# Weights of both layers in one shared pair of buffers, the second layer's prepared in the first layer's last units

## The chip, the cores and the metric

One core of a Trainium2 chip. The metric is the device time of one execution in microseconds, the median of several. Engines: PE (TensorE), DVE (VectorE), ACT (ScalarE), POOL (GpSimd) and SP (SyncE, which here only issues loads and stores).

## What is computed

Two transformer layers on 8 sequences of 256 tokens of 256 numbers, in float32:

```python
xn = _layernorm(x)
x = x + _L0_attn_ref(xn, ...) + _L0_ffn_ref(xn, ...)   # 32 query heads of 8, softmax, memory; 4-bit gated MLP of 2048
xn = _layernorm(x)
x = x + _L1_attn_ref(xn, ...) + _L1_ffn_ref(xn, ...)   # below; ternary gated MLP of 704

# _L1_attn_ref: xc = silu(causal conv of 4 taps over x)
q = _l2n((x @ Wq.T)...); k = _l2n((x @ Wk.T)...); v = _ln((x @ Wv.T)..., vn_g, vn_b)   # 16 heads of 16
i_gate = sigmoid(xc @ ig_w.T + ig_b); gamma = sigmoid(xc @ gamma_w.T + gamma_b)
_, mem = associative_scan(comb, (gamma, i_gate * k * v), axis=1)
o = groupnorm(_ln(mem, mn_g, mn_b) * q) * gn_g + gn_b
return (o * sigmoid(xc @ og_w.T + og_b)) @ Wo.T
# _L1_ffn_ref: quantized = clip(round(w / mean|w|), -1, 1); (sigmoid(x @ q1.T) * (x @ q2.T)) @ q3.T
```

## The kernel before

Float32 products are made of three products of halves: each operand is split into hi (a copy rounded to float32r) and lo (the exact value less hi), and hi*hi, hi*lo and lo*hi are added in PSUM. ACT makes the hi part, DVE or POOL the lo part.

**Layer 0** (`layer0`) runs as one loop over units u = -3 to 67, written out in every engine's queue. Unit u does the attention of head u % 8 of sequence u // 8 (64 in all) and one of 8 chunks of that sequence's MLP, one to three units later (`m = u - LAG`, `down_product(m - BEHIND)`). The weights of the MLP are decoded in the first units into `w_hi` and `w_lo`, [128, 8 pairs, 2, 768]; the last sequence's chunk m = 56 + a is the last reader of pair a. Per unit, PE makes turned scores (`scores_turned`, L832), gate and up (`hidden_product`, L735), scores for the maxima (`scores`, L807), probabilities times V (`weighted`, L847) and down (L874); DVE takes maxima (L595), splits them (`split_max`, L602 and L604), which SP then places by DMA (`place_max`, L251); ACT makes exponentials (L448), hid_hi (L458) and copies (L479); POOL makes hid (L347) and hid_lo (L341). In units 10 to 40 the ternary weights of the second layer are averaged, compared with a threshold and stored as signs (bf16) in `dram["signs"]`. After the last chunk of a sequence DVE adds down to X (step `mlp`, L585) and takes bn_stats (L588).

**Layer 1** (`layer1`) begins, in a block of its own (L985 to L1061), with what it needs once: SP loads the weights of the projections and gates (`l1w`, 1536 KB, L1001), the signs (L1002) and six small tensors (L1010); DVE makes bn_aggr of all 16 tiles, then the centring of the value columns (L1050 to L1056), POOL the reciprocal roots (L1021, L1023), ACT w_hi (L1036) and the ternary weights from the signs (`tern`, L1038) and three small ones (L1040 to L1042), DVE w_lo (L1058) and bias (L1060), POOL scales and wo_lo (L1028 to L1031). The engines meet at the end of each block. Semaphores are primed with 40 (`prime`) so that waits on "zero so far" have positive values.

Then a second block runs five turns, `turns(turn)`, with (late, early, ahead) = (None, 0, 1), (0, 1, 2), (1, 2, 3), (2, 3, None), (3, None, None); the numbers are groups of 512 tokens. I call them turns 0 to 4. In a turn, `ahead` is normalised (DVE, L1434), turned (PE `xn_turn`, L1644), split (ACT `xn_high`, DVE and POOL `xn_low`, L1156) and its convolution begun; `early` gets its projections (PE `query_key`, `value`, L1625; ACT `projected`), norms, gates and up products (`ffn_up`, L1678; ACT sigmoid L1288, DVE `hidden` L1478); `late` gets scan (DVE L1492), memory norm, down products, output norm (`output_normed`), output gate (`gated`, L1145 on POOL for one half and DVE for the other), turn (PE `o_turn`, L1744; ACT o_hi L1348; DVE o_lo L1547), output product (PE `output`, 24 products) and residual (DVE L1553). The queue of each engine is the order of the calls at the end of its `turn`. In PE's: b_turn, ffn_up(0), center_rows, query_key(0), (1), ffn_up(1), query_key(2), value, ... gamma(1), xn_turn(ahead, 0), gate(2), (3), xn_turn(ahead, 1), o_turn, output. On DVE:

```python
if ahead is not None:
    normalise(ahead)
if late is not None:
    output_normed()
if ahead is not None:
    xn_low(dve, ahead, 0)
if late is not None:
    gated(dve, late, 1)
```

## Time and profile before

| | us |
|---|---|
| median of 3 executions | 877.85 (875.49 to 878.04) |
| profiled execution | 876.82 |
| its span, first to last instruction | 874.9 |
| PE busy | 751.2 |
| DVE busy | 649.3 |
| ACT busy | 454.0 |
| POOL busy | 413.9 |
| layer 0, last instruction ends | 606.9 |
| turns begin | 625.5 |
| mean granted clock of TensorE, of full speed | 0.943 |

Times in the rows are microseconds from the first instruction of the profiled execution. A row of the timeline gives start, duration, engine, line, operation, output and inputs with their shapes, the count of merged instructions, and in brackets how long the engine had been idle before it and what released it. PEclk is the granted clock: 1.00 is 2.4 GHz, 0.50 is 1.2 GHz.

### The profile page before, as it was taken

To read this page: it belongs to the slowest core of one execution; us is meant where nothing else is said; L and a number is where in the kernel's file an instruction comes from. 1 tells how busy PE (TensorE), PEld (TensorE's weight loads), DVE (VectorE), ACT (ScalarE), POOL (GpSimd) and SP (SyncE) were. 2 spreads that over 40 slices of the span, in tenths; PEclk is the share of its full clock that TensorE was granted. 3 is DMA by queue.
4 is the path that set the end of the run, shared out by engine and by line. 5 is a ranking of instruction groups with operands and counts; after the bars stand their busy time and mean duration, and the time that the engine had idled before them with its cause. 6 is when DMAs were issued, how large, how long until landed. Compare 5 with 4: busy or idle time off the path is not lost. (4 is left out here: it accounts for less than half of the span.)

```text
span 874.9 us, 15195 instructions
## 1 busy us (share of the span) xinstructions
PE 751.2 (86%) x5602; PEld 648.0 (74%) x5602; DVE 649.3 (74%) x1122; ACT 454.0 (52%) x717; POOL 413.9 (47%) x335
## 2 busy tenths in 40 slices
PE   4268799999999999999999999996267987979773
PEld 3257688888888888888888888885156866858662
DVE  5989877787777677777687686653555898989966
ACT  4346645655756655655655665563554543545411
POOL 1344444254367467576344245334336273762832
PEclk9999999999999999999999999998588897979975
DMA  5011121201001111011000000001200000000000
GB/s 155 24 38 38 37 78 40 57 26 45 19 15 43 32 35 44 21 50 32 3 20 21 2 21 20 3 2 68 91 1 1 1 0 25 1 4 21 0 25 24
DMA packets 21388, 25.88 MB, mean 30 GB/s; under 512 B 4419, under 2 KB 17091, under 8 KB 21061
## 3 DMA queue, kind: packets, MB, share of 16 engines
q1 hardware_dynamic: 21316, 24.93, 9.7%
q8 instruction: 45, 0.74, 0.3%
q14 instruction: 27, 0.21, 0.1%
HBM read 14.83 MB, written 3.28 MB: 21 GB/s over the span
## 5 line engine op out<-in xcount | busy, mean ns | idle before, releaser
L595 DVE TENSOR_REDUCE neg_max<-s_pair 128x4 f32<-128x1024 f32 x127 | 154.9, 1220 | 76.4 <-PE s_pair L807 76.1
L448 ACT ACTIVATE probs<-t_pair 128x1024 f32<-128x1024 f32 x128 | 131.2, 1025 | 139.6 <-PE t_pair L832 139.4
L347 POOL TENSOR_TENSOR hid<-g,hid 128x512 f32<-128x512 f32 x64 | 82.1, 1283 | 179.0 <-DVE g L706 147.5
L341 POOL TENSOR_TENSOR hid_lo<-hid,hid_hi 128x512 fp32r<-128x512 f32 x64 | 85.4, 1335 | 99.0 <-ACT hid_hi L458 98.9
L807 PE MATMUL s_pair<-K,Q 96*128 96x256 f32 x508 | 85.2, 291 | 14.5 <-DVE neg_max L595 9.1
L807 PEld LDWEIGHTS s_pair<-K,Q 96*128 96x128 f32 x508 | 76.0, 195 | 23.1 <-issue 8.5
L832 PE MATMUL t_pair<-Q,K 104*128 104x512 f32 x256 | 85.8, 417 | 0.3 <-DMA Q<-max_parts 0.3
L874 PE MATMUL down<-w_hi,hid_hi 128*128 128x256 f32 x256 | 83.9, 328 | 0.7 <-POOL hid_lo L341 0.7
L874 PE MATMUL down<-w_lo,hid_hi 128*128 128x256 f32 x256 | 72.1, 282 | 0.0
L874 PE MATMUL down<-w_hi,hid_lo 128*128 128x256 f32 x256 | 72.1, 282 | 0.0
L1145 POOL TENSOR_TENSOR rows<-rows,par 128x512 f32<-128x512 f32 x24 | 35.1, 1464 | 75.7 <-DVE rows L1511 54.8
L847 PE MATMUL misc<-probs,V 128*32 128x256 f32 x1024 | 69.1, 388 | 1.5 <-DVE kc L565 1.0
L874 PEld LDWEIGHTS down<-w_hi,hid_hi 128*128 128x128 f32 x256 | 48.2, 188 | 26.4 <-issue 24.3
L735 PE MATMUL gate<-xn_hi,w_hi 128*128 128x256 f32 x256 | 57.0, 304 | 0.0
L698 DVE SCALAR_TENSOR_TENSOR g<-g,gate 128x512 f32<-128x512 f32 x64 | 42.8, 668 | 18.8 <-ACT g L461 18.7
L469 ACT ACTIVATE g<-g 128x512 f32<-128x512 f32 x64 | 40.2, 627 | 29.2 <-DVE g L698 29.2
L735 PE MATMUL up<-xn_hi,w_hi 128*128 128x256 f32 x256 | 52.6, 288 | 0.0
L735 PE MATMUL up<-xn_hi,w_lo 128*128 128x256 f32 x256 | 52.3, 287 | 0.0
L735 PE MATMUL up<-xn_lo,w_hi 128*128 128x256 f32 x256 | 52.2, 286 | 0.0
L735 PE MATMUL gate<-xn_hi,w_lo 128*128 128x256 f32 x256 | 51.4, 282 | 0.0
L735 PE MATMUL gate<-xn_lo,w_hi 128*128 128x256 f32 x256 | 51.3, 282 | 0.0
L735 PEld LDWEIGHTS gate<-xn_hi,w_hi 128*128 128x128 f32 x256 | 43.9, 192 | 6.8
(259 smaller groups left out, 1987.6 us busy)
## 6 DMA issues: line engine op xcount, KB each, us to landing
stage<-in_ternary SPq DMA_DIRECT2D x18, 256.0 KB, 2.8
Q<-q_hi SPq DMA_DIRECT2D x64, 64.0 KB, 2.0
stage<-in_scales SPq DMA_DIRECT2D x8, 384.0 KB, 3.4
X<-in_x SPq DMA_DIRECT2D x8, 256.0 KB, 3.8
Q<-q_lo SPq DMA_DIRECT2D x32, 64.0 KB, 2.0
Q<-max_parts SPq DMA_DIRECT2D x128, 4.0 KB
out<-X SPq DMA_DIRECT2D x8, 256.0 KB, 2.2
shared<-in_l1w SPq DMA_DIRECT2D x1, 1536.0 KB, 6.6
```

What stands on the lines that cost most here:

```text
L341: pool.tensor_tensor(hid_lo[:, m % 2, :, :].rearrange("p a n -> p (a n)"), hid[:, m % 2, :], hid_hi[:, m % 2, :, :].rearrange("p a n -> p ...
L347: pool.tensor_tensor(hid[:, m % 2, :], g[:, m % 2, :], hid[:, m % 2, :], ALU.mult).then_inc(S["hid_done"], 1)
L448: act.activation(probs[:, u % 2, th, :], t_pair[:], ACT.Exp, scale=SCALE).then_inc(S["probs_done"], 1)
L469: act.activation(g[:, m % 2, :], g[:, m % 2, :], ACT.Tanh, scale=GELU_B).then_inc(S["t_done"], 1)
L595: dve.tensor_reduce(neg_max[:, u % 2, 4 * jp:4 * jp + 4], score_banks(u, jp)[:].rearrange("p (s n) -> p s n", n=SEQ), AX_X, ALU.max, negat ...
L698: dve.scalar_tensor_tensor(out=g[:, m % 2, :], in0=g[:, m % 2, :], scalar=1.0, in1=gate[:], op0=ALU.add, op1=ALU.mult).then_inc(S["u_done" ...
L735: mm = pe.matmul(out, lhs[a][k], rhs[b][k], start=(n == 0), stop=(n == 3 * KC - 1))
L807: mm = pe.matmul(score_banks(u, jp)[:, 512 * j + SEQ * s:512 * j + SEQ * s + SEQ], Q[0:KROWS, quad, 2 * jp + j, P * s:P * s + P], K[0:KROW ...
L832: mm = pe.matmul(t_pair[:, 512 * jp:512 * jp + 512].rearrange("p (j n) -> p j n", j=2), K[rows, quad, hq, P * th:P * th + P], Q[rows, quad ...
L847: mm = pe.matmul(misc[32 * j:32 * j + 32, 0:SEQ], V[:, th, h, :], probs[:, u % 2, th, SEQ * j:SEQ * j + SEQ], start=(th == 0), stop=(th == ...
L874: mm = pe.matmul(down[:, D * t:D * t + D], h[:, m % 2, n, P * t:P * t + P], w[:, a, n, 2 * D:3 * D], start=(a == 0 and t == 0 and n == 0 a ...
L1145: ins = engine.tensor_tensor(*step)
```

## The change

Both layers use one pair of buffers, `keep["hi"]` and `keep["lo"]`. The second layer's projection weights lie in pairs 0 and 1, its ternary weights in pairs 2 to 4 of hi, and most of its split activations (xn_hi, xn_lo, xc_hi, xc_lo, h_hi, h_lo, wo_hi) in the rest. In layer 0's last units SP loads `l1w` in four pieces into buffers no longer used (unit 58), DVE centres the value columns (units 59, 60), ACT copies hi (units 60, 61), POOL subtracts lo (units 61 to 64), SP loads the signs in three pieces (unit 64, each behind the subtraction that frees its buffer), and ACT casts them (units 65 to 67). bn_aggr and the reciprocal root of each sequence but the last follow its `mlp` step. The first block of layer 1 is gone: the small loads are issued at the start of the turns' block, and the steps on them stand in turn 0's queues. Semaphores are no longer primed; waits for zero are left out.

Further, in the turns: `query_key` and `projected` of tiles 0 and 1 are called for `ahead` at the end of a turn (before o_turn on PE, after o_hi on ACT) and for group 0 at the start of turn 0; `normalise(ahead)` moves to behind `memory_normed` on DVE, its output lying in `mem_rows`; `output_normed` is parted, so that `xn_low` of ahead comes between its roots and their application (`output_applied`, whose body is the former end of `output_normed`); gamma(1) and its eviction come behind xn_turn(ahead, 0).

```diff
-        w_hi = sb("w2_hi", [P, PAIRS_N, 2, WORDS], F32R)
-        w_lo = sb("w2_lo", [P, PAIRS_N, 2, WORDS], F32R)
+        w_hi, w_lo = keep["hi"], keep["lo"]
...
-        q_neg = sb("q_neg", [P, 2, SEQ])
-        sigma = sb("sigma", [P, 2, SEQ])
+        queries = sb("queries", [P, 4, SEQ])
+        q_neg, sigma = queries[:, 0:2, :], queries[:, 2:4, :]
+        v_sum = sb("v_sum", [P, L1_HEADS])
...
+        def raw_piece(n):
+            return (stage[:, 0, :], stage[:, 1, :], queries[:].rearrange("p a n -> p (a n)")[:, 0:WORDS], w_stage[:])[n]
+
+        def sign_piece(i):
+            return raw_piece((0, 1, 3)[i]).bitcast(BF16)
...
-            sp.wait_ge(S["stored"], 16 * PIECES)
+                if u == NEXT_AT:
+                    sp.wait_ge(S["stored"], 16 * PIECES)
+                    sp.wait_ge(S["signed"], 3 * PIECES)
+                    sp.wait_ge(S["mem_mm"], 2 * BATCH)
+                    for n in range(4):
+                        sp.dma_start(raw_piece(n), dram["l1w"][:, n // 2, WORDS * (n % 2):WORDS * (n % 2) + WORDS]).then_inc(S["next_loaded"], 16)
+                if u == UNITS:
+                    for i, n in enumerate((1, 2, 4)):
+                        sp.wait_ge(S["next_lo"], n)
+                        sp.dma_start(sign_piece(i), dram["signs"][:, 2 * WORDS * i:2 * WORDS * i + 2 * WORDS]).then_inc(S["next_loaded"], 16)
...
+                elif kind == "mlp" and b < BATCH - 1:
+                    rs = keep["rstd"][:, 2 * b:2 * b + 2]
+                    pool.wait_ge(S["aggr_done"], 2 * b + 2)
+                    pool.tensor_scalar(rs, keep["mv"][:, 2 * b:2 * b + 2, 1], 1.0, EPS, ALU.mult, ALU.add).then_inc(S["pool_link"], 1)
+                    pool.wait_ge(S["pool_link"], linked())
+                    pool.tensor_tensor(rs, rs, half[:], ALU.pow)
+
+            def next_low(n):
+
+                pool.wait_ge(S["next_copied"], n + 1)
+                pool.tensor_tensor(w_lo[:, n // 2, n % 2, :], raw_piece(n), w_hi[:, n // 2, n % 2, :].bitcast(F32), ALU.subtract).then_inc(S["next_lo"], 1)
...
+                if 0 <= u - NEXT_AT - 3 < 4:
+                    next_low(u - NEXT_AT - 3)
...
+            def next_high(k):
+
+                act.wait_ge(S["next_centred"], k + 1)
+                act.wait_ge(S["down_done"], HEADS * (BATCH - 1) + k + 1)
+                for n in (2 * k, 2 * k + 1):
+                    act.activation(w_hi[:, k, n % 2, :], raw_piece(n), ACT.Copy).then_inc(S["next_copied"], 1)
+
+            def next_signs(i):
+
+                act.wait_ge(S["next_loaded"], 16 * 7)
+                act.wait_ge(S["down_done"], HEADS * (BATCH - 1) + 2 + i + 1)
+                act.activation(w_hi[:, 2 + i, :, :].rearrange("p a n -> p (a n)"), sign_piece(i), ACT.Copy).then_inc(S["next_copied"], 1)
...
+                if 0 <= u - NEXT_AT - 2 < KC:
+                    next_high(u - NEXT_AT - 2)
+                if 0 <= u - UNITS - 1 < 3:
+                    next_signs(u - UNITS - 1)
...
-                    linked(2)
+                    dve.wait_ge(S["dve_link"], linked(2))
+                    for t in range(2):
+                        dve.bn_aggr(keep["mv"][:, 2 * b + t, :], keep["stats"][:, 2 * b + t, :]).then_inc(S["aggr_done"], 1)
+
+            def next_centred(k):
+
+                columns = raw_piece(2 * k)[:, W_V:W_V + D].rearrange("p (h d) -> p h d", d=L1_DH)
+                dve.wait_ge(S["next_loaded"], 16 * 4)
+                dve.tensor_reduce(v_sum[:], columns, AX_X, ALU.add).then_inc(S["dve_link"], 1)
+                dve.wait_ge(S["dve_link"], linked())
+                dve.tensor_scalar(v_sum[:], v_sum[:], -1.0 / L1_DH, None, ALU.mult).then_inc(S["dve_link"], 1)
+                dve.wait_ge(S["dve_link"], linked())
+                mean = v_sum[:].rearrange("p (h a) -> p h a", a=1).to_broadcast([P, L1_HEADS, L1_DH])
+                dve.tensor_tensor(columns, columns, mean, ALU.add).then_inc(S["next_centred"], 1)
+                dve.wait_ge(S["next_centred"], k + 1)
...
+                if 0 <= u - NEXT_AT - 1 < KC:
+                    next_centred(u - NEXT_AT - 1)
...
-        shared = sb("shared", [P, KC * W_COLS])
+        shared = sb("shared", [P, 3 * KC * GT])
...
-        w_hi = sb("l1_hi", [P, KC, W_COLS], F32R)
-        w_lo = sb("l1_lo", [P, KC, W_COLS], F32R)
-        wo_hi = sb("wo_hi", [P, KC, D], F32R)
+        hi, lo = (keep[n][:].rearrange("p a b n -> p a (b n)") for n in ("hi", "lo"))
+        w_hi, w_lo = hi[:, 0:KC, :], lo[:, 0:KC, :]
+        split = lo[:, 5:8, :].rearrange("p a n -> p (a n)")
+        xn_hi, xn_lo, xc_hi, xc_lo = (split[:, KC * GT * n:KC * GT * n + KC * GT].rearrange("p (k n) -> p k n", k=KC) for n in range(4))
+        wo_hi = split[:, 4 * KC * GT:4 * KC * GT + KC * D].rearrange("p (k n) -> p k n", k=KC)
+        h_hi, h_lo = (x.rearrange("p a n -> p (a n)").rearrange("p (c n) -> p c n", n=GT) for x in (hi[:, 5:8, :], lo[:, 2:5, :]))
...
-        tern = sb("tern", [P, 3 * UPC], F32R)
+        tern = hi[:, 2:5, :].rearrange("p a n -> p (a n)")
...
-        half = sb("half", [P, TILES])
-
-
+        half = sb("half", [P, 2])
...
-        mv = sb("l1_mv", [P, TILES, 2])
-        rstd = sb("l1_rstd", [P, TILES])
+        mv, rstd = keep["mv"], keep["rstd"]
...
-        xn = osq[:].rearrange("p b n -> p (b n)").rearrange("p (t k n) -> p t k n", t=TPG, k=KC)
+        xn = mem_rows.rearrange("p (t k n) -> p t k n", t=TPG, k=KC)
...
+        wo_raw = flat(o[:, 0:2, :]).rearrange("p (k n) -> p k n", k=KC)
+        bias_raw = flat(vn[:, 0:2, :])
+        bias_b = o_hi[:, 0, :, :].rearrange("p k n -> p (k n)")
+        once = {n: ctx.enter_context(nc.semaphore(f"l1_{n}")) for n in "zeroed loaded scaled copied bias_done rstd_done".split()}
...
         def _(sp):
+            for dst, x in ((conv[:], dram["conv"]), (par[:], dram["scales_shifts"].partition_broadcast(P)), (gamma_b[:], dram["gamma_b"]),
+                           (const2[:], dram["const2"]), (wo_raw, dram["wo"])):
+                sp.dma_start(dst, x).then_inc(once["loaded"], 16)
+            sp.wait_ge(once["zeroed"], 1)
+            sp.dma_start(bias_raw[0:2, :], dram["gate_bias"]).then_inc(once["loaded"], 16)
...
-            pool.memset(xpad[:, :, :, 0:PAD], 0.0).then_inc(pad_zeroed, 1)
+            pool.memset(bias_raw, 0.0).then_inc(once["zeroed"], 1)
+            pool.memset(xpad[:, :, :, 0:PAD], 0.0).then_inc(once["zeroed"], 1)
+            pool.memset(half[:], -0.5).then_inc(once["zeroed"], 1)
+            pool.memset(eps16[:, 0:2 * PAIR_HEADS], 0.0).then_inc(once["zeroed"], 1)
+            pool.memset(eps16[:, 2 * PAIR_HEADS:3 * PAIR_HEADS], L1_DH * EPS).then_inc(once["zeroed"], 1)
+            last = slice(TILES - 2, TILES)
+            pool.tensor_scalar(rstd[:, last], mv[:, last, 1], 1.0, EPS, ALU.mult, ALU.add).then_inc(once["rstd_done"], 1)
+            pool.wait_ge(once["zeroed"], 5)
+            pool.wait_ge(once["rstd_done"], 1)
+            pool.tensor_tensor(rstd[:, last], rstd[:, last], half[:], ALU.pow).then_inc(once["rstd_done"], 1)
+
+            def scaled():
+                pool.wait_ge(once["loaded"], 16 * N_LOADS)
+                for n in (0, 2):
+                    scale = par[:, L1_DH * n:L1_DH * n + L1_DH]
+                    pool.tensor_scalar(scale, scale, 4.0, None, ALU.mult).then_inc(once["scaled"], 1)
+                pool.tensor_scalar(gn_g, gn_g, 4.0, None, ALU.mult).then_inc(once["scaled"], 1)
+                pool.wait_ge(once["scaled"], 3)
+                pool.wait_ge(once["copied"], 3)
+                pool.tensor_tensor(wo_lo[:], wo_raw, wo_hi.bitcast(F32), ALU.subtract).then_inc(once["scaled"], 1)
...
                     xn_low(pool, early, 1)
+                    scaled()
...
-            act.wait_ge(pad_zeroed, 1)
+            act.wait_ge(once["zeroed"], 2)
+
+            def constants():
+                act.wait_ge(once["loaded"], 16 * N_LOADS)
+                act.activation(ones_rows[:], const2[:, C2_E:C2_E + P], ACT.Copy).then_inc(once["copied"], 1)
+                act.activation(bias_b, bias_raw, ACT.Identity, scale=const2[:, C2_COL + 1:C2_COL + 2]).then_inc(once["copied"], 1)
+                act.activation(wo_hi, wo_raw, ACT.Copy).then_inc(once["copied"], 1)
...
                     xn_high(early, 0)
                     xn_high(early, 1)
+                    constants()
+                    projected(early, 0)
+                    projected(early, 1)
                 if early is not None:
...
                     hidden_high(0)
-                    projected(0)
-                    projected(1)
                     hidden(1)
-                    projected(2)
+                    projected(early, 2)
...
                     hidden(5)
-                    decays(1)
                 if ahead is not None:
                     xn_high(ahead, 0)
                 if early is not None:
+                    decays(1)
                     gate(2)
...
                 if late is not None:
                     for b in halves:
                         output_high(b)
+                if ahead is not None:
+                    projected(ahead, 0)
+                    projected(ahead, 1)
 
...
                     if g > 1:
-                        waiter(dve, g - 2)("s2_done", BPG)
+                        waiter(dve, g - 2)("mem_centered", BPG)
+                    if g == GROUPS - 1:
+                        dve.wait_ge(once["rstd_done"], 2)
...
+                    if late + 1 < GROUPS:
+                        waiter(dve, late + 1)("xn_turned", BPG)
...
                     inc(dve.tensor_tensor(s2[:], s2[:], rq[:], ALU.mult), "ro_done")
+
+                def output_applied():
+                    wait = waiter(dve, late)
...
                 if late is None:
+                    dve.wait_ge(once["zeroed"], 5)
                     normalise(early)
                     xn_low(dve, early, 0)
+                    dve.wait_ge(once["loaded"], 16 * N_LOADS)
                     convolve(early, range(0, 2))
+                    dve.wait_ge(once["copied"], 2)
+                    dve.scalar_tensor_tensor(out=bias[:], in0=bias_raw, scalar=const2[:, C2_COL:C2_COL + 1], in1=bias_b.bitcast(F32),
+                                             op0=ALU.mult, op1=ALU.add).then_inc(once["bias_done"], 1)
+                    dve.wait_ge(once["bias_done"], 1)
+                    dve.wait_ge(once["scaled"], 3)
...
                 if late is not None:
                     memory_normed()
+                if ahead is not None:
+                    normalise(ahead)
                 if early is not None:
                     hidden(1)
...
-                if ahead is not None:
-                    normalise(ahead)
                 if late is not None:
                     output_normed()
                 if ahead is not None:
                     xn_low(dve, ahead, 0)
                 if late is not None:
+                    output_applied()
                     gated(dve, late, 1)
...
-                def query_key(t):
-                    wait = waiter(pe, early)
+                def query_key(g, t):
+                    wait = waiter(pe, g)
                     wait("xn_hi_done", t // 2 + 1)
                     wait(f"xn_lo_done{t // 2}", 1)
                     if t >= 2:
                         wait("qk_sq", t - 1)
-                    else:
-                        wait("gates_done", 0)
+                    elif g > 0:
+                        waiter(pe, g - 1)("gates_done", t + 3)
...
+                    if early == 0 and t == 0:
+                        pe.wait_ge(once["copied"], 1)
+                        pe.wait_ge(once["bias_done"], 1)
...
+                    if late == 0:
+                        pe.wait_ge(once["scaled"], 4)
...
                     xn_turn(early, 0)
                     xn_turn(early, 1)
+                    query_key(early, 0)
+                    query_key(early, 1)
...
                 if early is not None:
-                    query_key(0)
-                    query_key(1)
                     ffn_up(1)
-                    query_key(2)
+                    query_key(early, 2)
...
                     ffn_up(5)
-                    gamma(1)
                 if ahead is not None:
                     xn_turn(ahead, 0)
                 if early is not None:
+                    gamma(1)
                     gate(2)
                     gate(3)
                 if ahead is not None:
                     xn_turn(ahead, 1)
+                    query_key(ahead, 0)
+                    query_key(ahead, 1)
                 if late is not None:
                     for b in halves:
...
+            "mv": sb("l1_mv", [P, TILES, 2]),
+            "rstd": sb("l1_rstd", [P, TILES]),
+            "hi": sb("hi", [P, PAIRS_N, 2, WORDS], F32R),
+            "lo": sb("lo", [P, PAIRS_N, 2, WORDS], F32R),
```

The removed block is printed above (L985 to L1061).

## Rows read from the trace of the kernel before

**Rows 1.** The page's first part: busy us (share of the span) xinstructions.
```profile
PE 751.2 (86%) x5602; PEld 648.0 (74%) x5602; DVE 649.3 (74%) x1122; ACT 454.0 (52%) x717; POOL 413.9 (47%) x335
```

**Rows 2.** Stretches: length, busy time by engine, PEclk, DMA share, GB/s.
```profile
400.00:500.00 100.00, 100.00 (x854) 87.19 (x853) 73.45 (x134) 60.38 (x96) 43.62 (x38) 1.00 0.06 16
...
605.50:625.50 20.00, 0.00 (x0) 0.00 (x0) 8.24 (x26) 8.03 (x5) 9.65 (x11) 0.56 0.45 173
...
734.50:789.00 54.50, 47.03 (x249) 39.93 (x250) 49.63 (x87) 24.75 (x44) 30.72 (x22) 0.91 0.03 10
```

**Rows 3.** Timeline of DVE, in the gap.
```profile
614.00 0.69 DVE L1050 TENSOR_REDUCE v_sum<-shared 128x32 f32<-128x512 f32 x1 [5.42 <-DMA shared<-in_l1w]
...
614.93 0.76 DVE L1056 TENSOR_TENSOR shared<-shared,v_sum 128x256 f32<-128x256 f32 x2
```

**Rows 4.** Timelines of DVE, ACT and POOL in layer 0's last units.
```profile
568.39 0.28 DVE L602 CAST max_parts<-misc 8x128 fp32r<-8x128 f32 x1 [0.63 <-PE misc L819]
...
569.74 0.69 DVE L698 SCALAR_TENSOR_TENSOR g<-g,gate 128x512 f32<-128x512 f32 x1 [0.75 <-ACT g L461]
...
575.26 1.03 ACT L448 ACTIVATE probs<-t_pair 128x1024 f32<-128x1024 f32 x1 [2.38 <-PE t_pair L832]
...
576.88 1.29 POOL L341 TENSOR_TENSOR hid_lo<-hid,hid_hi 128x512 fp32r<-128x512 f32 x1 [3.38 <-ACT hid_hi L458]
...
584.57 1.30 POOL L341 TENSOR_TENSOR hid_lo<-hid,hid_hi 128x512 fp32r<-128x512 f32 x1 [3.38 <-ACT hid_hi L458]
```

**Rows 5.** By line: count, ns min/median/max; and a load, KB, us to landing.
```profile
L351 POOL TENSOR_TENSOR w_lo<-w_stage,w_hi x8: 1804/1834/2110, 21.8 to 104.5; 128x768 fp32r<-128x768 f32 x8
...
L440 ACT ACTIVATE w_hi<-w_stage x8: 829/838/844, 20.9 to 102.7; 128x768 fp32r<-128x768 f32 x8
...
stage<-in_scales SPq DMA_DIRECT2D x5, 384.0 KB, 3.5
```

**Rows 6.** Timelines of POOL and DVE at the end of layer 0.
```profile
602.33 1.27 POOL L341 TENSOR_TENSOR hid_lo<-hid,hid_hi 128x512 fp32r<-128x512 f32 x1 [0.98 <-ACT hid_hi L458]
...
606.11 0.75 DVE L588 BATCH_NORM_STATS2 stats<-X 128x6 f32<-128x256 f32 x2
```

**Rows 7.** Timelines of POOL, ACT and DVE: the gap's start, casts and end.
```profile
607.37 0.52 POOL L1015 MEMSET bias_raw<- 128x512 f32 x1 [3.76 <-POOLq L117]
...
618.39 4.03 ACT L1038 ACTIVATE tern<-rows 128x4608 fp32r<-128x4608 bf16 x1
...
625.49 0.73 DVE L1434 TENSOR_SCALAR osq<-X,l_mv,l_rstd 128x256 f32<-128x256 f32 x2 [1.48 <-PEq L985]
```

**Rows 8.** Timelines of ACT and PE, turn 0.
```profile
629.57 1.28 ACT L1288 ACT_TABLE_LOAD   x1
...
631.06 1.19 PE L1678 MATMUL lbank<-l_xn_hi,tern 128*128 128x512 f32 x2 [2.81 <-POOL l_xn_lo L1156]
...
634.85 0.60 ACT L1288 ACTIVATE sig<-lbank 128x512 f32<-128x512 f32 x1 [4.00 <-PE lbank L1678]
...
637.64 0.62 PE L1678 MATMUL lbank<-l_xn_hi,tern 128*128 128x512 f32 x2
```

**Rows 9.** Timelines of DVE and PE, turn 1.
```profile
678.49 1.26 DVE L1492 TENSOR_TENSOR_SCAN rows<-shared,lbank 128x256 f32<-128x256 f32 x2 [2.37 <-PE lbank L1728]
...
721.40 1.76 DVE L1156 TENSOR_TENSOR l_xn_lo<-xpad,l_xn_hi 128x512 fp32r<-128x512 f32 x1
...
725.68 1.97 PE L1744 MATMUL lbank<-ident,rows 128*128 128x128 f32 x8 [4.75 <-POOL rows L1145]
...
733.73 0.69 DVE L1553 TENSOR_TENSOR X<-lbank,X 128x512 f32<-128x512 f32 x1 [1.87 <-PE lbank L1625]
```

**Rows 10.** The chain that ended last, turn 1: start, us, what.
```profile
728.20 5.50 PE lbank L1625 x24
```

**Rows 11.** Stretches of 2 us around idle times of PE, turn 1.
```profile
704.00:706.00 2.00, 0.77 (x5) 0.51 (x5) 1.93 (x5) 0.00 (x0) 2.00 (x2) 1.00 0.00 0
...
724.00:726.00 2.00, 0.32 (x2) 0.32 (x3) 1.97 (x4) 0.14 (x1) 1.55 (x2) 0.50 0.00 0
```

108 lines of the change are left out of this document (15 added, 93 removed).

## The prediction

> **What bounds the kernel now.** The page first: TensorE (PE) is busy for 86% of the span [rows 1], an average over stages that the table by stretches takes apart [rows 2]. In layer 0 (400 to 500 us) PE is busy for 100.00 of 100 us: work added to VectorE (DVE), ScalarE (ACT) or GpSimd (POOL) there costs nothing while it stays inside their idle time. From 605.50 to 625.50 PE does nothing; DVE, ACT and POOL have 8 to 10 us of work each, one after another, beside 173 GB/s of loads. From 625.50 on a second layer runs in five turns. The first is a chain through all engines; in turn 2 (734.50 to 789.00) DVE is busy for 49.63 of 54.5 us, so DVE sets the pace and only its waits, or instructions of its own that get shorter, can be won. So I read three places: the end of layer 0, the gap, and the waits of DVE in turns 1 to 3.
>
> **Layer 0's last units (58 to 67).** A unit is 7.7 us long, the distance of two hid_lo on POOL [rows 4]. The change adds:
> - SP: four loads of 384 KB at unit 58, behind the row placement for unit 59. The next placement is a unit later. The same 1536 KB were there for DVE at 614.00, 6.6 us after the block's start [rows 3, 7], inside a unit. The three waits ahead of the loads are on work done by unit 57. Cost 0.
> - DVE: at units 59 and 60 a sum, a scaling and an addition. Half of the 0.69 us sum, half of the 0.76 pair [rows 3] and a short scaling are about 1.0 us a unit. Queued behind is the split of the row maxima, before which DVE idles 0.63 us, and behind that 0.75 us more [rows 4]: 1.0 against 1.38. Cost 0.
> - ACT: at units 60 and 61 two copies of 768 columns, 0.84 us each [rows 5], ahead of an exponential before which ACT idles 2.38 us [rows 4]. Cost 0.
> - POOL: at units 61 to 64 one subtraction of 768 columns, 1.83 us each [rows 5]. The first fits into 3.38 us of idle time [rows 4], the second nearly as well; the third delays a hid_lo that PE wants some us later. The fourth starts when POOL is free at 601.35 and ends at 603.2, where the last hid_lo started at 602.33 [rows 6]: the last products, and DVE's end of the layer at 606.86 [rows 6], come 0.85 us later. The small steps per batch (two bn_aggr, a POOL power of two columns) lie beside PE's 100%.
> - The last load of signs waits for that fourth subtraction. A load of 384 KB took 3.5 us to land [rows 5], so 606.7. ACT waits for all three loads before three casts, together of the columns of the one that took 4.03 us [rows 7]; with 0.1 for the splitting 610.8. No cover is left: DVE is done at about 608, and ACT becomes the engine that ends the layer.
>
> **The gap.** Before, the second layer's turns began at 625.49 [rows 7]. After, their block starts 0.5 us behind the last engine (606.86 to 607.37 before, [rows 6, 7]): 611.3. Term A = 611.3 - 625.45 = -14.15. Bounds: a landing of 2 us, which small loads need by the page, and of 5, towards the 6.6 of four times the bytes: -15.7 to -12.6. I take 3.5, the load of equal size.
>
> **Turn 0** (times from the block's start). DVE now waits for five memsets (0.9 in place of 0), so the transposes and both halves of xn come 0.9 later; six loads, about 0.5 us of issue each, land at about 5 to 6.4. PE's queue has query_key(0), query_key(1) and then ffn_up(0). PE is cold: after the idle time eight products of 512 columns took 3.55 us, 631.06 to 634.61, 0.44 each; then it is at the upper level [rows 8]. Twelve of them from 5.0 on are 5.3, so 10.3; ffn_up(0) at full clock 1.9 more, 12.2. ACT copies and squares query_key(1) until 11.5, and only then comes the load of the sigmoid's table, 1.28 us, which lay in idle time before [rows 8]: 12.8. Sigmoid 0.60, product 0.69: ffn_up(1) starts at 14.0, where it started at 637.64 - 625.45 = 12.2 [rows 8]. The rest of the turn hangs on that chain. Term B = +1.8; bounds +1.2 (PE at full clock one product earlier) and +2.8 (loads land late, DVE's four taps and the new bias step behind them).
> A page speaks against this place. The Trainium skill, "ScalarE: Activation LUTs", section "What ACT_TABLE_LOAD costs", adds a drain of 1.38 us to each load of 1.28; by it the sum would be 1.4 higher, an estimate of 861.9. The row shows only the 1.28, because 4.00 us of idle time follow it.
>
> **Turn 1** (59.6 us). DVE waits seven times, 8.2 us in all: 2.37, 1.89 and 0.21 at its start, 0.94 before the sum of squares, 0.73 and 0.16 for o_hi and 1.87 at the end (the first and the last in [rows 9]). (1) normalise(ahead) moves forward at the same length: 0. (2) xn_low(ahead) moves ahead of the handover to POOL: its 1.76 us [rows 9] beside POOL's L1145 become 0.69, as in turn 0, -1.07; in exchange POOL's three steps start later against DVE, and the wait for o_hi grows by 0.9. (3) query_key 0 and 1, 2.8 us at full clock, leave PE's queue ahead of ffn_up(1) and fill the 4.75 us in which PE idled before o_turn [rows 9]: the 0.94 goes. They need gate(3)'s eviction and xn_low, both there before, so the o_turn queued behind isn't held. (4) The clock. After that idle time it is granted at 0.50 [rows 11], and the 24 output products take 5.50 us [rows 10] where the upper level needs half, 2.8. After an idle time of 1.23 us it stayed at 1.00 [rows 11]. Afterwards PE idles about 1.1, transposes for 1.0 and idles 1.1 more, between the two rows. At 2.4 GHz the 1.87 goes; at 1.2 it stays. (5) At the start PE idles 3 us, four transposes within, where it idled 5.50, and POOL's last two steps come 0.5 us sooner against DVE; the 2.1 us for the squares goes only if PE is at 2.4 GHz. Low level at both places: -1.7. Outputs at the upper one: -3.6. Both: -5.3. Term C = -2.7, the middle of the first two, since the idle times lie between the rows.
>
> **Turn 2** (54.5 us): the same without (5), and 0.48 us in place of 0.94. -0.8 at the low level, -2.7 at the upper; term D = -1.8. **Turn 3**: nothing ahead, only 0.45 us of wait goes: E = -0.45. **Turn 4**: 0.
>
> **Sum:** -14.15 + 1.8 - 2.7 - 1.8 - 0.45 = -17.3. The profiled run took 876.82 us (span 874.9 and 1.9 around it), after 859.5. The median of the three runs, 877.85, is 1.0 higher: 860.5.
>
> **Rivals.** (a) PE stays at 2.4 GHz throughout: B 1.5, C -5.3, D -2.7, -21.1: 856.7. For it: the idle time before o_turn falls from 4.75 to near 1; against: only short transposes lie between two such times. (b) PE low at every tail, loads late: A -12.6, B +2.8, C -1.7, D -0.8, E 0, -12.3: 865.5. (c) The table's load has a tail which the 4.00 us of idle time behind it hid: between 0 and 4.0, at its middle +2.0: 862.5. (d) The change doesn't take the preparation off the path: ACT's and POOL's queues are served late, and three subtractions (5.5 us) and the casts (4.0) still follow 606.86: A about -8, 867 and up. Against: the idle times in [rows 4]. (e) Slower: the additions don't fit into the units. PE's product with V waits for split maxima; DVE's slack ahead of them is 1.38 us. If the wait for the loads or DVE's share exceeds that, units 59 to 65 stretch. It takes 2.9 us in each of seven to eat 17.3 and the 2.6 beyond which it can be told: over 880.5. Against: 1.0 against 1.38, and a whole unit for the loads to land.
>
> **How the numbers follow.** Forecast 0.42, (a) 0.20, (b) 0.20, (c) 0.08, (d) 0.07, (e) 0.03. 854.5 (a, with the signs landing in 2) to 867 (b, 1.5 over its centre) hold 8 in 10: outside lie (d), (e) and the edges of (a) and (b). The likeliest case alone is 858 to 863. A measurement here tells 0.3%, 2.6 us, from no change. Faster 0.95; the upper edge of (d) gives the same, 0.02; slower 0.03.
>
> **What would show it.** In the profile after: the second layer's turns begin near 611 (A), with ACT's three casts right ahead and DVE idle; units 59 to 63 still 7.7 us long (if longer, e); 1.28 us of table load right ahead of the first sigmoid, and ffn_up(1) 14 us into the block (B; at 16, c); PEclk and the length of the 24 output products, 2.8 or 5.5 us, in turns 1 and 2 (C, D); xn_low on DVE at 0.69. The prediction is wrong if another engine than ACT ends layer 0, or if DVE's waits don't fall in turns 1 and 2, from 8.2 and 3.4 us.

## The result, and the profile after

The kernel after takes 866.31 us (median of four executions, 861.46 to 866.79), beside 876.67 for the kernel before on the same chip: ratio 0.987, 95% interval 0.985 to 0.989. It is faster by 1.3%, where 2.0% was forecast: about 10.4 us instead of 17.3. Five more executions, made with the last experiments, took 862.14 to 867.25 (ratio 0.9872, 0.985 to 0.989).

Of the page's first part (busy us, share of the span, instructions) little moved [before: rows 1]: the work is the same, and DVE has 4.6 us more of it.

```profile
PE 750.2 (87%) x5602; PEld 645.5 (75%) x5602; DVE 653.9 (76%) x1123; ACT 454.8 (53%) x722; POOL 420.1 (49%) x353
```

The end of layer 0 and the gap in the profile after. Timelines of POOL, DVE and ACT, from the fourth subtraction to the first instruction of layer 1's block (start us, duration us, engine, line, operation, out<-in, count, and in brackets the idle time ahead and what ended it):

```profile
601.43 1.84 POOL L354 TENSOR_TENSOR lo<-w_stage,hi 128x768 fp32r<-128x768 f32 x1
603.23 1.72 POOL L360 TENSOR_TENSOR hid_lo<-hid,hid_hi 128x512 fp32r<-128x512 f32 x1
...
601.47 2.35 DVE L619 TENSOR_TENSOR X<-X,att 128x512 f32<-128x512 f32 x1
...
608.19 0.25 DVE L629 BATCH_NORM_AGGREGATE l_mv<-stats 128x2 f32<-128x6 f32 x2
...
606.42 2.86 ACT L482 ACTIVATE hi<-stage 128x1536 fp32r<-128x1536 bf16 x2 [4.05 <-DMA w_stage<-signs]
609.18 1.47 ACT L482 ACTIVATE hi<-w_stage 128x1536 fp32r<-128x1536 bf16 x1
...
610.92 0.53 POOL L1190 MEMSET rows<- 128x512 f32 x1 [5.98 <-POOLq L109]
```

ACT ends layer 0 at 610.65, 2.2 us behind DVE's last step, after three casts for which it waited 4.05 us. The block of layer 1 begins at 610.92; before, the turns began at 625.49 [rows 7]. The units ahead of this kept their 7.7 us.

Turn 0, timelines of ACT and PE:

```profile
622.19 1.28 ACT L1293 ACT_TABLE_LOAD   x1
623.49 0.60 ACT L1293 ACTIVATE sig<-lbank 128x512 f32<-128x512 f32 x1
...
624.86 1.43 PE L1702 MATMUL lbank<-lo,hi 128*128 128x512 f32 x5 [1.97 <-DVE l_hid L1489]
```

PE's second up product of the MLP, ffn_up(1), starts 13.94 us into the block, where the prediction had 14.0, with the table's load right ahead of the first sigmoid [before: rows 8]. The sigmoid starts 0.02 us behind the load's end, and the load 0.02 us behind the square ahead of it (621.58 to 622.17): no tail on either side.

The turns themselves. Stretches from one turn's first scan to the next's, first of the kernel before, then of the kernel after: length, busy time of PE, PEld, DVE, ACT and POOL (instructions), PEclk, DMA share, GB/s.

```profile
674.85:734.43 59.58, 49.27 (x248) 41.48 (x248) 49.91 (x87) 24.87 (x44) 34.11 (x25) 0.86 0.02 5
734.43:788.90 54.47, 46.93 (x249) 39.83 (x249) 49.60 (x86) 24.75 (x44) 30.72 (x22) 0.91 0.03 10
788.90:840.63 51.73, 45.59 (x240) 38.72 (x240) 42.78 (x77) 22.69 (x40) 28.70 (x21) 0.90 0.03 11
```

```profile
610.92:662.92 52.00, 40.33 (x168) 32.15 (x168) 31.22 (x48) 27.05 (x48) 23.89 (x26) 0.84 0.06 14
662.92:721.75 58.83, 48.51 (x249) 40.34 (x250) 52.23 (x87) 26.03 (x47) 33.17 (x25) 0.91 0.00 1
721.75:776.31 54.56, 46.53 (x248) 39.29 (x248) 52.05 (x87) 24.75 (x44) 29.61 (x22) 0.94 0.04 15
776.31:829.62 53.31, 44.56 (x228) 37.97 (x228) 42.78 (x79) 20.85 (x36) 28.27 (x21) 0.87 0.03 11
```

With turn 0 at 49.40 and turn 4 at 34.27 us before (34.38 after), the ledger is, in us:

| | forecast | measured |
|---|---|---|
| A, start of the turns | -14.15 | -14.53 |
| B, turn 0 | +1.8 | +2.60 |
| C, turn 1 | -2.7 | -0.75 |
| D, turn 2 | -1.8 | +0.09 |
| E, turn 3 | -0.45 | +1.58 |
| turn 4 | 0 | +0.11 |
| sum | -17.3 | -10.9 (874.9 to 864.0) |

So 5.9 of the 6.4 us that are missing were expected in turns 1 to 3 (turn 0 is 0.8 too long and A 0.4 better than said). In turns 1 and 2 DVE's idle time did fall, from 9.67 to 6.60 and from 4.87 to 2.51 (length less DVE's busy time), more than the prediction asked (1.6 and 0.7). But DVE's busy time rose by 2.32 and 2.45 with the same number of instructions, where it was to fall by 1.07. These are the instructions that grew, in turn 1. Timelines of DVE before, then of DVE and POOL after:

```profile
714.49 2.69 DVE L1434 TENSOR_SCALAR osq<-X,l_mv,l_rstd 128x256 f32<-128x256 f32 x4
...
725.74 0.99 DVE L1446 TENSOR_SCALAR shared<-xpad,conv 128x512 f32<-128x512 f32 x2
```

```profile
678.41 4.46 DVE L1445 TENSOR_SCALAR rows<-X,l_mv,l_rstd 128x256 f32<-128x256 f32 x4
...
709.37 0.69 DVE L1129 TENSOR_TENSOR lo<-xpad,lo 128x512 fp32r<-128x512 f32 x1
...
713.97 2.86 DVE L1457 TENSOR_SCALAR shared<-xpad,conv 128x512 f32<-128x512 f32 x2
...
678.57 2.77 POOL L1118 TENSOR_TENSOR rows<-rows,par 128x512 f32<-128x512 f32 x2 [12.09 <-DVE rows L1524]
681.41 1.30 POOL L1118 TENSOR_TENSOR rows<-rows,q_kept 128x512 f32<-128x512 f32 x1
...
713.87 1.27 POOL L1118 TENSOR_TENSOR rows<-rows,gates 128x512 f32<-128x512 f32 x1
715.09 1.46 POOL L1135 TENSOR_TENSOR lo<-l_hid,hi 128x512 fp32r<-128x512 f32 x1
```

normalise(ahead) went from 2.69 to 4.46 us (it takes 1.38 in turn 0), the first two taps from 0.99 to 2.86, and xn_low fell from 1.76 [rows 9] to 0.69. Each of the long ones lies beside GpSimd's work, as the next experiments test.

In turn 3, PE and DVE of the profile after:

```profile
783.19 2.55 PE L1702 MATMUL lbank<-lo,hi 128*128 128x512 f32 x8 [2.39 <-DVE l_hid L1489]
785.53 1.05 PE L1649 MATMUL lbank<-hi,lo 128*128 128x512 f32 x2
...
793.63 0.69 DVE L1489 TENSOR_TENSOR l_hid<-sig,lbank 128x512 f32<-128x512 f32 x1 [2.02 <-ACT sig L1293]
```

PE now idles 2.39 us for hidden(0) ahead of ffn_up(1), and two products of 512 columns behind it take 1.05 us, where two take 0.62 at full clock. DVE then waits 2.02 us, where it waited 0.45. The clock falls behind the idle time and not in it: it is granted at 1.00 up to 784 us and at 0.50 from 786 on. Stretches of 2 us of the kernel after:

```profile
784.00:786.00 2.00, 2.00 (x8) 1.57 (x7) 1.81 (x7) 0.23 (x1) 0.00 (x0) 0.67 0.00 0
786.00:788.00 2.00, 2.00 (x6) 1.61 (x5) 1.97 (x5) 0.37 (x1) 1.29 (x1) 0.50 0.00 0
```

### The profile page after: what moved, and what is told of

Read it like the earlier page. It is cut to its first block and busy times, and to the rows that moved or that the text cites. A ratio compares the mean times of both kernels' runs of the same rounds, so it can differ in the third digit from the quotient of the medians.

```text
span 864.0 us, 15139 instructions
## 1 busy us (share of the span) xinstructions
PE 750.2 (87%) x5602; PEld 645.5 (75%) x5602; DVE 653.9 (76%) x1123; ACT 454.8 (53%) x722; POOL 420.1 (49%) x353
## 5 line engine op out<-in xcount | busy, mean ns | idle before, releaser
L928 PE MATMUL down<-hi,hid_hi 128*128 128x256 f32 x256 | 84.0, 328 | 1.9 <-POOL hid_lo L360 1.9
L928 PE MATMUL down<-lo,hid_hi 128*128 128x256 f32 x256 | 71.9, 281 | 0.0
L928 PE MATMUL down<-hi,hid_lo 128*128 128x256 f32 x256 | 71.7, 280 | 0.0
L928 PEld LDWEIGHTS down<-hi,hid_hi 128*128 128x128 f32 x256 | 48.1, 188 | 27.9 <-issue 24.9
L1702 PE MATMUL lbank<-lo,hi 128*128 128x512 f32 x192 | 54.7, 431 | 12.6 <-DVE l_hid L1489 12.3
L789 PE MATMUL gate<-xn_hi,hi 128*128 128x256 f32 x256 | 57.0, 304 | 0.0
L1649 PE MATMUL lbank<-hi,lo 128*128 128x512 f32 (+1 forms) x192 | 53.3, 378 | 1.2 <-DVE lo L1129 1.2
L789 PE MATMUL up<-xn_hi,hi 128*128 128x256 f32 x256 | 52.2, 286 | 0.0
L789 PE MATMUL up<-xn_lo,hi 128*128 128x256 f32 x256 | 51.9, 285 | 0.0
L789 PE MATMUL up<-xn_hi,lo 128*128 128x256 f32 x256 | 51.9, 285 | 0.0
```

The source lines that it names most:

```text
L789: mm = pe.matmul(out, lhs[a][k], rhs[b][k], start=(n == 0), stop=(n == 3 * KC - 1))
L928: mm = pe.matmul(down[:, D * t:D * t + D], h[:, m % 2, n, P * t:P * t + P], w[:, a, n, 2 * D:3 * D], start=(a == 0 and t == 0 and n == 0 a ...
L1649: mm = pe.matmul(dst, lhs[a](k), rhs[b](k), start=(n == 0), stop=(last and n == 3 * KC - 1))
L1702: mm = pe.matmul(banks[bank][:], w[:, k, P * c:P * c + P], x[:, k, :], start=(n == 0), stop=(n == 3))
```

## The experiments

All kernels but e15_after are the kernel after with small edits; times are medians of four or five executions, ratios are to the kernel before, run beside them (876.5 to 876.9).

**e1_norm: normalise(ahead) where GpSimd is idle**

```diff
+                if ahead is not None:
+                    normalise(ahead)
                 if late is not None:
                     memory_normed()
-                if ahead is not None:
-                    normalise(ahead)
```

> The kernel after, with one edit: VectorE's normalise(ahead) stands ahead of memory_normed, while GpSimd is idle, in place of behind it, beside GpSimd's three steps of memory_scaled. Theory P (the two engines get in each other's way): the four instructions take 1.38 us in turns 1 and 2, as in turn 0, in place of 4.46. Of the 3.1 us saved some 1.9 a turn reach the end, since hidden(2) can't come earlier than about 11.1 us after hidden(0) (turn 3: 782.46 to 793.63), which leaves a wait of about 1.2 ahead of it: turns 1 and 2 each 1.9 shorter, 862.5 us in all against 866.3. Rival T (the instructions are slower because they now write to the tile of the memory rows in place of the squares' tile, or because of what they read): they stay at about 4.4 us, turns 1 and 2 keep 58.8 and 54.6, and the time stays at 866.

Measured: 859.47 us, ratio 0.981 (0.979 to 0.984), 6.8 us below the kernel after. Turn 1, timelines of DVE and POOL, and then the stretches of turns 1 and 2:

```profile
671.78 1.38 DVE L1445 TENSOR_SCALAR rows<-X,l_mv,l_rstd 128x256 f32<-128x256 f32 x4
...
676.72 2.69 POOL L1118 TENSOR_TENSOR rows<-rows,par 128x512 f32<-128x512 f32 x2 [10.93 <-DVE rows L1524]
```

```profile
662.23:717.04 54.81, 45.02 (x248) 38.21 (x248) 49.71 (x88) 25.90 (x47) 33.79 (x25) 0.97 0.01 4
717.04:768.75 51.71, 45.08 (x249) 37.95 (x250) 49.36 (x87) 24.65 (x44) 30.23 (x22) 0.97 0.02 7
```

The same four instructions with the same operands take 1.38 us: the tile isn't it (rival T falls), what GpSimd does at the same time is. DVE's busy time is 2.5 and 2.7 us lower. The turns are 4.0 and 2.8 us shorter where 1.9 each was expected. In turn 2 nearly all of this is the busy time; in turn 1 DVE's idle time also fell, by 1.5 us, with PE's clock granted at 0.97 in place of 0.91. That the clock did this part wasn't tested.

The Trainium skill, "SBUF — State Buffer", sections "SBUF: two separate sides" and "Who interferes with whom", says that VectorE and GpSimd share one pair of SBUF ports, held for a whole instruction by the one that starts first, while the other stands still; VectorE wants it for copies and scalings in its two-port modes, and for two SBUF inputs against a GpSimd instruction that reads SBUF. The rows agree: one piece of normalise takes 0.40 us alone and up to 1.47 beside GpSimd, xn_low and X + att (two SBUF inputs) 0.69 alone and 1.76 and 2.35 beside it, while hidden, with one input in PSUM, keeps its 0.68 everywhere.

**e2_hid0: hidden(0) between two taps**

```diff
                 if early is not None:
-                    convolve(early, range(2, TAPS))
+                    if late is not None:
+                        convolve(early, range(2, 3))
+                        hidden(0)
+                        convolve(early, range(3, TAPS))
+                    else:
+                        convolve(early, range(2, TAPS))
                 if late is not None:
                     memory_summed()
-                if early is not None:
+                elif early is not None:
                     hidden(0)
```

> The kernel after, with one edit: in turns 1 to 3 VectorE's hidden(0) stands between the third and the fourth tap, in place of behind the taps and the sums of the memory's squares. Theory H (with the query and key products gone from the queue, TensorE's ffn_up(1) stands right behind ffn_up(0) and waits 2.4 us for hidden(0)): this wait falls to near 0 and in turn 3, where nothing covers it, VectorE's wait of 2.02 us ahead of hidden(2) goes: turn 3 is 2.0 shorter (53.3 to 51.3). Turns 1 and 2 stay within 0.5, since VectorE has work of its own all the time between hidden(0) and hidden(2). In all -2.0: 864.3. Rival C (TensorE's clock is what makes turn 3 longer; its eight products took 2.55 us in place of 2.0): the wait ahead of hidden(2) falls by 0.5 at most, 866.

Measured: 862.48 us, ratio 0.985 (0.983 to 0.987), an interval that overlaps that of the kernel after: the gain is shown for turn 3, not for the whole. Turn 3 is 50.66 us long, PE's ffn_up(1) follows center_rows with no idle time, and DVE has no wait ahead of hidden(2). Turns 1 and 2: 58.16 and 54.82. The turn behaves as theory H says. But rival C isn't out by this run: another profile of the unchanged kernel after (e15_after, below) has the same idle time and yet no low clock behind it. Timelines of PE and DVE in its turn 3:

```profile
781.92 2.12 PE L1702 MATMUL lbank<-lo,hi 128*128 128x512 f32 x8 [2.40 <-DVE l_hid L1489]
...
790.79 0.69 DVE L1489 TENSOR_TENSOR l_hid<-sig,lbank 128x512 f32<-128x512 f32 x1 [0.45 <-ACT sig L1293]
```

The eight products take 2.12 us and DVE waits 0.45. So the 2.02 us are two things: 0.45 without a fall of the clock, and about 1.6 more where it falls behind the new idle time. In e2_hid0, without the idle time, neither is there.

**e3_qkback: the query and key products back in their own turn**

```diff
 # PE
                     xn_turn(ahead, 1)
-                    query_key(ahead, 0)
-                    query_key(ahead, 1)
 ...
                 if early is not None:
+                    if late is not None:
+                        query_key(early, 0)
+                        query_key(early, 1)
                     ffn_up(1)
 # ACT: projected(0), projected(1) likewise, ahead of hidden(1)
```

> The kernel after, with the query and key products 0 and 1 of turns 1 to 3, and ScalarE's copies of them, back in the turn that uses them, behind center_rows, where the kernel before has them. Theory H: TensorE has 2.8 us of work again while it waits for hidden(0), and turn 3 is 1.6 us shorter (wait ahead of hidden(2) 0.4 in place of 2.0); in turns 1 and 2 TensorE is idle for some 4 us ahead of o_turn again, the output products are at 1.2 GHz, and the wait for them returns from 0.2 and 1.0 to 1.9: up to +1.7 and +0.9. Net between -1.6 and +1.0, 864.7 to 867.3, with the three turns moving against each other. Rival, the prediction's step (3): the products' place in the turn costs 0.94 and 0.48 of wait ahead of hidden(2) in turns 1 and 2 and 0.45 in turn 3, and moving them back gives +1.9 beside the outputs' part: 868 or more.

Measured: 865.5 us, ratio 0.988 (0.986 to 0.990), the same as the kernel after within what can be told. Turn 3 is 50.92 long and its wait 0.46; turns 1 and 2 are 58.77 and 55.03, with 1.64 and 1.22 us of waits for the output products, which take 4.80 and 4.46 us in place of 3.07 and 4.58. Turns 1 and 2 moved less than theory H allowed. The prediction's step (3), as a gain of its own, falls: 868 or more was its price.

**e4_weights: the weights' move alone**

The edit puts turns 1 to 3 back as in the kernel before: on DVE normalise(ahead) behind output_summed and xn_low behind output_applied, on PE and ACT the products 0 and 1 as in e3_qkback, and gamma(1) ahead of xn_turn(ahead, 0).

> The kernel after, with everything that it changed in turns 1 to 3 put back as in the kernel before: normalise(ahead) behind output_summed, xn_low(ahead) behind output_applied, query and key products 0 and 1 in their own turn, gamma(1) ahead of xn_turn(ahead, 0). What is left is the move of the weights into layer 0's last units and turn 0's new start. Theory (the gap's and turn 0's terms were right, and the moves within the turns bring nothing): turns 1, 2 and 3 have 59.6, 54.5 and 51.7 us as before, the turns' block starts at 610.9 and turn 0 has 51 to 52, so 876.7 - 14.5 + 2.2 = 864.4, 1 to 2 below the kernel after. Rival (the moves within the turns are worth the 4.95 us of the prediction, and the loss sits in turn 0 or in layer 0): about 871, 5 above the kernel after.

Measured: 862.96 us, ratio 0.984 (0.983 to 0.986); its interval overlaps that of the kernel after by 0.0009. Turns 1, 2 and 3 take 59.92, 53.09 and 50.93. The moves within the turns are thus worth between nothing and a loss of some 3 us; a gain of 4.95 is out. What the change wins, it wins at the gap.

**e14_lowback: xn_low(ahead) behind output_applied again**

```diff
-                if ahead is not None:
-                    xn_low(dve, ahead, 0)
                 if late is not None:
                     output_applied()
+                if ahead is not None:
+                    xn_low(dve, ahead, 0)
+                if late is not None:
                     gated(dve, late, 1)
```

> The kernel after, with one edit: VectorE's xn_low(ahead) stands behind output_applied again, as in the kernel before, beside GpSimd's gated(late, 0). Theory P (what moves is only which instruction meets GpSimd's): xn_low takes 1.76 us again in place of 0.69, the two first taps 1.0 in place of 2.86, and the 0.9 us of waits for o_hi ahead of output_low return: turns 1 and 2 within 0.6 us of those of the kernel after (58.8 and 54.6), the time within 1 us of its. Rival, the prediction's step (2) (the swap is worth 1.07 us in each of the two turns): 2 us slower than the kernel after.

Measured: 862.7 us, ratio 0.985 (0.983 to 0.987), 2.9 us below e15_after of the same chip. Timeline of DVE, turn 1:

```profile
709.99 1.76 DVE L1129 TENSOR_TENSOR lo<-xpad,lo 128x512 fp32r<-128x512 f32 x1
...
714.33 1.00 DVE L1457 TENSOR_SCALAR shared<-xpad,conv 128x512 f32<-128x512 f32 x2
715.97 1.29 DVE L1563 TENSOR_TENSOR o_lo<-lbank,o_hi 128x512 fp32r<-128x512 f32 x2 [0.64 <-ACT o_hi L1353]
```

The instructions trade as expected: xn_low +1.07, taps -1.86, wait +0.64, with +0.29 for the taps behind o_low (2.68 for 2.39), a sum of +0.14. So step (2) wins nothing by these rows: where one instruction leaves GpSimd's company, the next one enters it. Turn 2 is 53.90 us, 0.66 shorter. That the median is 2.9 us lower, where within 1 us was expected, isn't explained by these rows. The two intervals overlap, but its four executions are all within 861.9 to 863.7, so it may be more than chance. One thing differs for PE: its idle time of 1.4 us lies ahead of the query and key products, which then run right up to o_turn, where the kernel after idles 1.3 us directly ahead of o_turn. The output products of turns 1 and 2 run at full clock here (3.08 and 3.13 us). Whether this is the cause wasn't tested.

**e7_singly and e8_singly_lows: the end of layer 0**

```diff
 # e7: one semaphore for each load of signs
-                act.wait_ge(S["next_loaded"], 16 * 7)
+                act.wait_ge(S[("x_first", "x_rest", "next_loaded")[i]], (32, 16 * EARLY, 16 * 5)[i])
 # e8: that, and on POOL
-                if 0 <= u - NEXT_AT - 3 < 4:
-                    next_low(u - NEXT_AT - 3)
+                for n in {3: (0,), 4: (1,), 5: (2, 3)}.get(u - NEXT_AT, ()):
+                    next_low(n)
```

On SP, not shown, each of the three loads of signs counts on the semaphore of its own cast.

> The kernel after, with one edit: each of ScalarE's three casts of the signs waits for its own load alone, in place of all three loads. In the kernel after the first two loads land some 15 and 10 us before the layer's end, and ScalarE idles 4.05 us for the third before it does all three casts (606.42 to 610.65), two of which take 2.86 us. Theory (ScalarE ends layer 0, as the prediction says): the first two casts move into ScalarE's idle time, the third ends at about 607.9, VectorE's last step at 608.44 ends the layer, and the turns' block starts at about 608.9 in place of 610.9: -2.0, 864.3. Rival (something else holds the start of the second layer's block, as the loads or the memsets): the start moves by less than 0.5, 866.

> As e7_singly, and GpSimd's fourth subtraction (next_low(3)) is done right behind the third, a unit earlier, so that it isn't in front of the last hid_lo. In the kernel after the last subtraction delays the last hid_lo, TensorE waits 1.94 us for it, and VectorE's att addition beside it takes 2.35 us where it took 0.67. Theory (the two engines' shared access to SBUF and GpSimd's queue order cost the end of layer 0 about 1.3 us): VectorE's last step comes at about 607.1 in place of 608.44 and the block starts at 607.6, 3.3 us before that of the kernel after: 863.0. Rival (two subtractions of 1.84 in one unit don't fit into its 3.38 us of idle time, and that unit is longer by what is missing, 0.3, or by a whole hid_lo, 1.3): the start is at 607.9 to 608.9, no better than e7_singly.

Measured: e7_singly 861.7 us, ratio 0.983 (0.982 to 0.984), 2.6 us below what was expected; e8_singly_lows 862.86, ratio 0.984 (0.982 to 0.986). Executions differ by some 3 us already (over all kernels the first subtraction starts between 579.4 and 582.7) in where the last units lie, so the start of the block is measured from the first subtraction. POOL's timelines of the kernel after, of e7_singly and of e8_singly_lows:

```profile
581.31 1.84 POOL L354 TENSOR_TENSOR lo<-stage,hi 128x768 fp32r<-128x768 f32 x1
```

```profile
579.39 1.84 POOL L354 TENSOR_TENSOR lo<-stage,hi 128x768 fp32r<-128x768 f32 x1
...
606.82 0.52 POOL L1190 MEMSET rows<- 128x512 f32 x1 [3.79 <-POOLq L109]
```

```profile
581.16 1.84 POOL L354 TENSOR_TENSOR lo<-stage,hi 128x768 fp32r<-128x768 f32 x1
...
607.38 0.52 POOL L1190 MEMSET rows<- 128x512 f32 x1 [3.79 <-POOLq L109]
```

29.61 us in the kernel after, 27.43 in e7_singly (-2.18; expected -2.0) and 26.22 in e8_singly_lows (-3.39; expected -3.3). In e8_singly_lows the last hid_lo takes 1.28 us again, DVE's X + att 0.69, and DVE ends layer 0 at 607.09. Both steps did what was said, and ACT's casts ended the layer in the kernel after. The medians of the two can't be told apart, since their intervals overlap and the turns behind differ between executions by more than the 1.2 us in question (turn 3 took 53.30 in the one profile and 51.13 in the other): that e8_singly_lows is the faster is shown for the gap, not for the whole.

**e5_both: normalise and hidden(0) together**

> The kernel after, with the edits of e1_norm and e2_hid0 together: normalise(ahead) ahead of memory_normed, and hidden(0) between the third and the fourth tap in turns 1 to 3. In e1_norm VectorE still waited 0.73 us (turn 2) and 0.25 + 1.04 us (turn 3) for sigmoids, on the chain that starts with hidden(0). Theory (the two costs add up: the stretched normalise, 3.1 us in each of two turns, and TensorE's wait for hidden(0)): these waits go, 1 to 2 us below e1_norm's 859.5, so 857.5 to 858.5. Rival (with normalise at 1.38 us and early, the hidden chain has its place anyway): 859.5 as e1_norm.

Measured: 856.68 us, ratio 0.977 (0.976 to 0.979), 2.8 us below e1_norm, with no wait of DVE left in turn 2 and none ahead of hidden(2) in turn 3: the two costs add up.

**e11_warm: unread products in PE's idle time**

```diff
+                if late is not None and early is not None:
+                    if ahead is None:
+                        waiter(pe, early)("gates_done", TPG)
+                    else:
+                        waiter(pe, early)("hid_done", FFN_CHUNKS)
+                    for _ in range(14 if ahead is None else 4):
+                        pe.matmul(banks[2 if ahead is None else 6][:], w_hi[:, 0, 0:P], w_hi[:, 0, 0:512], start=True, stop=True)
                 if late is not None:
                     for b in halves:
                         o_turn(b)
```

> The kernel after, with products added whose result nobody reads: in TensorE's idle time ahead of o_turn, four products of 512 columns in turns 1 and 2 and 14 in turn 3, so that its idle time there falls from 1.3 and 4.5 us to under 0.5. Theory (the idle time ahead of o_turn is what lowers TensorE's clock for the 24 output products): they take about 3.1 us in all three turns, where the kernel after has 3.07, 4.58 and 5.49 in turns 1, 2 and 3; turn 2 is 1.0 and turn 3 2.0 to 2.4 shorter: 863 in all. Rival (the idle times between o_turn and the output products, 0.6 to 1.3 us, are enough to lower the clock, or the products of the next turn's start then run at the low level in their place): the three turns together stay within 1 us of 166.7, and the time at 866.

Measured: 861.1 us, ratio 0.983 (0.981 to 0.984), 4.5 to 5.2 us below the two medians of the kernel after. Stretches of 2 us of the kernel after, around o_turn of turn 3, then PE's timeline and the stretches at the same place in e11_warm:

```profile
818.00:820.00 2.00, 0.00 (x0) 0.00 (x0) 1.84 (x3) 0.29 (x3) 1.84 (x3) 0.70 0.00 0
820.00:822.00 2.00, 1.05 (x5) 1.05 (x6) 0.00 (x0) 0.54 (x1) 2.00 (x2) 0.50 0.00 0
```

```profile
813.79 3.47 PE L1830 MATMUL lbank<-hi 128*128 128x512 f32 x14 [0.69 <-ACT gates L1338]
817.67 1.09 PE L1771 MATMUL lbank<-ident,rows 128*128 128x128 f32 x8 [0.40 <-POOL rows L1118]
```

```profile
816.00:818.00 2.00, 1.60 (x9) 1.06 (x8) 0.52 (x1) 0.63 (x1) 1.92 (x3) 1.00 0.00 0
818.00:820.00 2.00, 1.03 (x9) 0.79 (x8) 1.01 (x2) 1.08 (x2) 2.00 (x2) 1.00 0.00 0
```

The clock stays at 1.00 (2.4 GHz) and doesn't fall to 0.50 (1.2 GHz). The 24 output products take 3.06, 3.13 and 3.11 us in the three turns, where the kernel after has 3.07, 4.58 and 5.49; turns 1 to 3 sum to 162.0 us, 4.7 below 166.7, where the rival allowed 1. The 0.97 to 1.30 us between o_turn and the outputs didn't lower it. Turn 4 gave 0.5 us back (34.91 for 34.38): its output products took 5.48 us for 4.88.

**e15_after, e9_all and e12_all_warm: the kernel after again, and everything together**

e9_all has the edits of e5_both and e8_singly_lows, and one more line on ACT; e12_all_warm adds the products of e11_warm.

```diff
             act.wait_ge(once["zeroed"], 2)
+            act.activation(sig[0:2, 0, 0:2], xpad[0:2, 0, 0, 0:2], ACT.Sigmoid)
```

> The kernel after itself, unchanged, for a firmer mean beside the other runs: its four first runs were 861.46, 865.88, 866.74 and 866.79. If the differences between runs are a matter of where TensorE's clock rises and falls against the program, the new runs spread over the same 5 us and the mean over all is about 865; if the 861.46 was a lone outlier, they lie at 865.9 to 866.8.

> All edits that paid together, on the kernel after: normalise(ahead) ahead of memory_normed, hidden(0) between the third and fourth tap, ScalarE's casts each behind its own load, the fourth subtraction a unit earlier, and a sigmoid of 2 x 2 elements as ScalarE's first instruction of the second layer, so that the table's load stands in idle time. From e5_both's 856.7: the end of layer 0 gives 3.4 less (2.2 and 1.2, measured against the same point of layer 0), the table 0.5, since the taps on VectorE end 0.54 us ahead of hidden(0): 852.8. Rival (VectorE then waits in turn 0 for the six loads, which are issued at the block's start and don't come earlier against it): 853.3, with hidden(0) of turn 0 as far behind the block's start as before.

> e9_all with the unread products of e11_warm ahead of o_turn in turns 1 to 3. If TensorE's level in these three places is worth what e11_warm showed (output products 3.1 us in place of 3.1 to 5.5), turns 1 to 3 together are 2 to 3 us shorter than in e9_all: 850.5. Rival (part of the gain is only luck of the level's phase, and turn 4 gives it back, whose products ran at the low level in e11_warm, 5.5 us in place of 4.9): 1 us or less below e9_all.

Measured: e15_after 865.57 us (862.14 to 867.25), a spread again and no lone outlier. e9_all 855.3, ratio 0.975 (0.973 to 0.977); hidden(0) of turn 0 starts 12.40 us into the block in place of 13.20, so the table's load did leave the chain, but the whole is 2.5 us above the sum that was expected, and its interval overlaps that of e5_both (0.976 to 0.979): what the end of layer 0 and the table add to e5_both isn't shown in the whole. Its output products are wholly or mostly at the low level in all three turns, 4.52, 5.50 and 5.49 us. e12_all_warm 848.66, ratio 0.969 (0.967 to 0.971), 6.6 us below e9_all where 2 to 3 were expected, with 3.06, 3.10 and 3.09. The stretches of turns 1 to 3, of e9_all and then of e12_all_warm:

```profile
658.95:714.82 55.87, 46.34 (x248) 39.07 (x248) 49.52 (x88) 26.05 (x47) 33.75 (x25) 0.94 0.01 4
714.82:767.73 52.91, 46.14 (x248) 39.37 (x248) 49.42 (x88) 24.78 (x44) 30.18 (x22) 0.94 0.04 12
767.73:819.05 51.32, 43.37 (x228) 37.00 (x228) 42.78 (x77) 20.85 (x36) 28.60 (x21) 0.90 0.03 11
```

```profile
658.62:713.39 54.77, 46.21 (x253) 38.45 (x254) 49.49 (x87) 26.04 (x47) 33.81 (x25) 0.97 0.00 0
713.39:764.31 50.92, 44.90 (x253) 37.44 (x254) 49.29 (x87) 24.78 (x44) 30.24 (x22) 1.00 0.04 11
764.31:812.81 48.50, 43.23 (x242) 36.13 (x242) 42.65 (x78) 20.75 (x36) 28.67 (x21) 1.00 0.04 14
```

DVE's busy time is the same in both to 0.3 us; the rest of the 5.9 us (160.1 to 154.2) is idle time of DVE that went with the low clock. e12_all_warm is the fastest of all: 17.7 us below the kernel after, 27.9 below the kernel before.

## Why the prediction was right or wrong

**Right.** Faster was right, and 866.31 lies in the range, 0.7 us inside its upper end; the likeliest case (858 to 863) doesn't hold it. The end of layer 0 went as worked out, step by step: the units kept their length, the fourth subtraction delayed the last hid_lo (DVE's last step at 608.44, forecast "about 608"), ACT's casts ended the layer, and A was 0.4 us off. In e15_after, the same kernel, all of this lies some 1.6 us earlier, so the start alone can't be compared that closely; counted from the same hid_lo of each profile (584.57 us before, 584.71 after, 582.98 in e15_after), A is -14.7 and, in e15_after, -14.5. DVE's waits fell, as was said, from 8.2 to 5.0 and from 3.4 to 1.2 us in turns 1 and 2. e7_singly and e8_singly_lows confirm both causes by taking them away. B was right up to ffn_up(1) (13.94 against 14.0). The other 0.8 us of turn 0 lie behind it: over the kernels with this turn 0 unchanged it took 50.9 to 53.0 us, some near 50.9 and most near 52.2, so one profile can't settle them.

**Wrong: C, step (1), "normalise(ahead) moves forward at the same length: 0".** This is the main failure. The step took the duration of a row (2.69 us) to the new place, though that row was itself stretched; alone it is 1.38 us, beside GpSimd's three steps of memory_scaled 4.46. That is 1.8 us more of DVE's busy time in each of two turns, 3.5 in all, beside 6.4 missing. e1_norm, which brings the 1.38 back, is 6.8 us faster. The prediction used the same effect in step (2), in its favour, and didn't ask what each moved instruction would meet.

**Wrong: C and D, step (2), the 1.07 us of xn_low.** The instruction did fall to 0.69. But the taps, which then lay beside GpSimd's later steps, rose by 1.87, and covered the waits for o_hi that the prediction had growing by 0.9. e14_lowback shows the trade at +0.14 by its rows, none of the gain.

**Wrong: E, and (3) in part, "the 0.94 goes".** It took the query and key products as work in front of ffn_up(1). They were work beside a wait: ffn_up(1) needs hidden(0), which DVE reaches only behind the taps and the sums. With the products gone, PE idles 2.4 us and nothing is sooner: turn 3 keeps the 0.45 us that were to go (e15_after), and in the profile after the clock fell behind that idle time and the wait became 2.02. In turns 1 and 2 the wait did go, but since normalise(ahead) now stands there; e2_hid0 and e5_both show that moving hidden(0) is what frees PE.

**Right in kind, not to be given as one number: (4), the clock.** Where the idle time ahead of o_turn was filled, in e11_warm and e12_all_warm, the output products were at the upper level in all six turns. Where 1.3 to 1.4 us of it were left, in turns 1 and 2 of eight profiles, they took 3.07 to 3.11 us in four of 16 turns and 4.41 to 5.50 in twelve. In the profile after, turn 1 was at the upper level (3.07 us) and turn 2 mostly at the lower (4.58); in e15_after, the same program, 4.60 and 4.62. The forecast's middle between the two levels was fair for a mean, not for any one profile. The upper level is 3.07, where the prediction had half of 5.50.

**Not right in the profile after: (5), the start of turn 1.** At the low level DVE's wait for the squares was to fall by 0.5 from 2.1 us; it was 2.6 with PE at 0.50 from 666 to 672 us, and 1.3 in e15_after. One more slip is small: for turn 2 the terms named add up to -0.65 and -2.5, where the prediction has -0.8 and -2.7.

**The rivals.** 865.5 of rival (b) is the number that was measured, but not its mechanism: the loads landed at 5.1 us, the early end, and A was better than it said. (a) fell with the low clock in turns 2 and 3. (c) fell with the 0.02 us behind the table's load; the estimate of 861.9 with it, which rests on the drain that the Trainium skill, "ScalarE: Activation LUTs", section "What ACT_TABLE_LOAD costs", adds: no run here shows one. (d) and (e) fell with A and the units' 7.7 us. None of them contained the stretched instructions: all five kept DVE's busy time in the turns fixed or falling, and that was the number that rose.

## What to carry to other kernels

When an instruction is moved, price it by what runs on the neighbouring engine at the new place, not by its old duration: look up its shortest instance first, and ask what moves into the place that it leaves. Work taken out of an in-order queue is a gain only if the instruction behind it was ready; here it had covered a wait, and the idle time that took its place lowered TensorE's clock in some executions. Unread products in such idle times were worth 4.5 to 6.6 us here, about half of the change itself.

## What the runs showed of the hardware that was not expected

- A four-instruction scaling on VectorE took 1.38, 2.69 or 4.46 us by what GpSimd did beside it, with the same operands; an addition of two SBUF tiles 0.69 or 2.35. GpSimd's own instructions stretch less: its subtraction hid_lo 1.27 to 1.72.
- The same idle time of TensorE, 2.4 us at the same place of the same program, with products up to it and behind it, was followed by a granted clock of 0.50 in one profile and of 1.00 in another. Nine executions of the kernel after spread over 5.8 us (861.46 to 867.25), more than half of what the change brought; that this clock is the whole cause of the spread was not tested.
- Idle times of 1.0 to 1.3 us between o_turn and the output products didn't lower a clock of 1.00 (e11_warm, e12_all_warm), while the 4.5 us ahead of o_turn in turn 3 lowered it in each profile that had them (output products of 4.65 to 5.49 us in place of 3.1).
